# Top-32 selection of two heads in turns, with the check of the counts threaded through the next chunk maxima

## The chip, the cores and the metric

The kernel runs on one core of one Trainium2 chip. The metric is the device time of the whole program in microseconds (us), the median over runs. The engines are PE (TensorE: matrix products and transposes), DVE (VectorE), ACT (ScalarE), POOL (GpSimd) and SP (which only issues transfers). Each has its own instruction stream in program order, and they meet through semaphores.

## The reference, cut to what matters

One layer in three parts: a cross attention from 128 text rows to 2048 context rows with a state-space filter behind it, a banded self attention, and a mixture of 16 experts. The change lies in the first part, which is computed for 4 batches and 4 heads, so for 16 heads in all:

```python
scores = jnp.einsum('bthd,bghd->bhtg', Q, K) / np.sqrt(DH)     # 128 x 2048 for one head
topv, topi = jax.lax.top_k(scores, K_TOP)                      # K_TOP = 32
probs = jax.nn.softmax(topv, axis=-1)
attn = jnp.zeros_like(scores).at[bi, hi, ti, topi].set(probs)
attn_mean = attn.mean(axis=1)                                  # over the 4 heads of a batch
```

Beside it, the filter needs powers exp(dt * A * l) of complex numbers for 128 lags, as sines and exponentials of outer products.

## The kernel before, in words

The 16 heads go in order of batch; heads 2m and 2m+1 are pair m, so there are 8 pairs, and two pairs are a batch. For pair m the engines do this:

- PE multiplies queries and keys (`scores`, L1280), ACT copies the products from PSUM to SBUF (`scores`, L591) into one of five score buffers SC.
- DVE takes the 8 largest of each of 32 chunks of 64 scores (`chunk_maxima`, 32 MAX8 at L949), then finds the 32 largest of these 256 candidates (`threshold`: four MAX8 of 256 at L958, three MATCH_REPLACE8 at L961 between them). The 32nd is the head's threshold.
- `threshold` ends with two counts over the 128 partitions: how many candidates reach the threshold (L965), and in how many chunks the eighth one does (L966). A chunk of which all eight reach it could hide a ninth. `settle` (after the second head of a pair) brings the counts to one number: four reductions of 32 partitions each (L972), a maximum, a 32x32 transpose, a maximum; DVE reads the word into a register, and branches to an exact selection if it is above 64. With these inputs it never is. Then the memset at L985 signals `topk`.
- ACT waits for `topk` and runs `exponentials(m)` (L603): eight small instructions for the normalisation, then one exponential of 128 x 2048 for each head into W[0] and W[1] (L618). Each signals `e_done`.
- DVE runs `masked(i)` (L987): (score >= threshold) * exponential, 128 x 2048, one SCALAR_TENSOR_TENSOR at L990. It signals `masked`, which releases the score buffer and the next step.
- POOL adds the heads of a batch (`add_head`, L429 and L434, two TENSOR_TENSOR of 1024 columns for heads 1, 2 and 3 of a batch).

The powers of the filter are threaded through the same streams, one quarter q for each batch: ACT makes phases (`lag_turns`, `step_turns`), DVE rounds them (`whole(q)`, L997 and L998), POOL takes the fractions (`fractions(q)`, L442 and two at L444), ACT takes sines (L658, L659, each side of a table load), `lag_sizes` (L666) and `step_sizes` (L673), POOL multiplies (`magnitudes(q)`: L450, two transfers that swap the halves, L455, L456) and combines (`powers(q)`: L464 to L466; the last quarter is on DVE, `last_powers`, L1056 to L1058), PE contracts (`lags(q)`, L1338), and DVE gathers (`diagonal(q)`, L1004 and L1006). `step_turns(q)` waits until `lags(q-1)` has read the buffer that it writes.

The order on each engine is written out by hand. DVE, before, for heads i = 0 to 17: `chunk_maxima(i)`; `whole` (at i = 1, 6, 10, 14); `masked(i-2)`; `diagonal` (at i = 7, 11, 15); `threshold(i)`; and `settle` if i is odd. `last_powers` stands before `masked(14)`. POOL, for i = 2 to 17: `powers(i/4-1)` (at i = 4, 8, 12); `add_head(i-2)`; `fractions` (at i = 6, 10, 14); `magnitudes` (at i = 3, 7, 11, 15). At i = 16, `gains(0)` (L471, L472, which wait for ACT's `text_norm(0)` behind the last exponentials) stand before `add_head(14)`. ACT, for odd m: `exponentials(m-1)`, scores, attended rows, sines, sizes; for even m: exponentials, scores, context keys, `lag_turns`, `step_turns`, context keys.

Every instruction of `threshold` and `settle` is followed by a wait for its own end (`link`):

```python
def __call__(self, ins):
    self.n += 1
    ins.then_inc(self.sem, 1)
    self.eng.wait_ge(self.sem, self.n)
```

## Time and profile before

| what | value |
| --- | --- |
| time, median of 3 runs | 776.48 us (775.92 to 777.83) |
| the profiled execution, its own time | 782.62 us |
| its span | 780.8 us |
| PE, DVE, ACT, POOL busy over the span | 87%, 48%, 35%, 29% |
| DVE busy, 50 to 250 us | 43.41, 42.88, 45.64 and 42.67 us of each 50 |
| ACT busy, 50 to 250 us | 37.62, 42.06, 39.93 and 37.66 us of each 50 |
| POOL busy, 50 to 250 us | 43.67, 37.31, 35.36 and 38.00 us of each 50 |
| granted TensorE clock, 50 to 250 us | 0.67, 0.81, 0.70 and 0.66 |

The shares over the span mix three parts of the kernel. The selection lies in the first 255 us; the rest of the span belongs mainly to PE. Busy time says how full an engine is, not which one the others wait for.

### The profile page before, as it was taken

The numbers are of one execution on the slowest core, as the hardware profiler recorded it, in microseconds if no ns is written. First come the engines' busy times: TensorE is split into PE (matmuls) and PEld (weight loads), VectorE is DVE, ScalarE is ACT, GpSimd is POOL, SyncE is SP. The second block draws the span as 40 slices with busy tenths as digits, with TensorE's granted clock in tenths as the row PEclk, the third lists the DMA queues.
The fourth block names the chain that finished last, engine by engine and source line by source line (L and its number), as shares of the span: only waits on it lengthen the run. The fifth ranks groups of instructions, "written<-read, shape, count | busy, mean of one in ns | idle before, by whom it ended". The sixth has DMA issues, their size and how long they took to land.

```text
span 780.8 us, 10116 instructions
## 1 busy us (share of the span) xinstructions
PE 681.5 (87%) x3848; PEld 320.2 (41%) x3848; DVE 374.8 (48%) x1179; ACT 273.1 (35%) x580; POOL 227.5 (29%) x146
## 2 busy tenths in 40 slices
PE   4948659878478799999999999989799999999997
PEld 2314235334244354444444444545554333333343
DVE  5988879998997335561002341534662111001114
ACT  1867868879778110013120001545111001111010
POOL 2479767856957920000000000000140000000012
PEclk9976677868568899999999999999799999999999
DMA  9971320702704851006005014001958999999923
GB/s 289 292 280 40 107 82 7 263 1 83 281 0 161 264 222 40 1 0 216 0 7 209 0 39 177 1 1 47 384 199 303 389 375 346 372 373 369 382 80 126
DMA packets 63521, 132.94 MB, mean 170 GB/s; under 512 B 8368, under 2 KB 18544, under 8 KB 62960
## 3 DMA queue, kind: packets, MB, share of 16 engines
q1 hardware_dynamic: 59072, 122.91, 43.6%
q0 software_dynamic: 1920, 6.29, 2.8%
q10 hardware_dynamic: 2480, 3.08, 1.2%
q8 instruction: 30, 0.49, 0.3%
q14 instruction: 19, 0.16, 0.1%
HBM read 121.86 MB, written 8.32 MB: 167 GB/s over the span
## 4 chain that ended last, share of the span: by engine, by line
PE 63%; DVE 16%; POOL 9%; ACT 6%; issue 3%; DMA 2%; ACTq 0%; DVEq 0%; POOLq 0%
PE PS L1675 8%; PE PS L1650 7%; PE PS L1471 7%; PE PS L1491 7%; PE PS L1389 6%; PE PS L1243 4%; DVE KA L949 4%; PE PS L1508 4%; PE PS L1670 4%; PE PS L1655 4%; DVE AR L990 2%; PE PS L1505 2%; POOL TT L434 2%; PE PS L1319 1%; DVE V L958 1%
## 5 line engine op out<-in xcount | busy, mean ns | idle before, releaser
L415 POOL TENSOR_TENSOR RS<-VE,CST 128x1 f32<-128x1 f32 (+1 forms) x18 | 11.2, 621 | 268.7 <-DVE VE L912 266.4
L1276 PE MATMUL PS<-AR,WK 128*128 128x512 f32 x96 | 54.7, 726 | 17.3 <-DMA AR<-in_ctxT 17.3
L949 DVE MAX8 KA<-AR 128x8 f32<-128x64 f32 x512 | 66.4, 210 | 2.4 <-issue 2.0
L1214 DVE COPY AR<-PS 128x512 f32<-128x512 f32 (+1 forms) x9 | 5.9, 668 | 124.3 <-PE PS L1243 124.3
L1675 PE MATMUL PS<-AR,TT 128*32 128x512 f32 x512 | 60.3, 593 | 1.5 <-issue 1.4
L567 POOL DMA_INDIRECT AR<-expert_rows,SLU x8 | 8.3, 1034 | 181.0 <-DMA expert_rows<-XT 178.9
L1650 PE MATMUL PS<-AR 128*32 128x512 f32 x512 | 57.9, 594 | 0.9 <-ACT AR L863 0.6
L1471 PE MATMUL PS<-TT,AR 128*128 128x512 f32 (+2 forms) x144 | 55.5, 546 | 3.3 <-ACT TT L791 3.3
L1293 PE MATMUL PS<-AR,QT 32*128 32x512 f32 x128 | 43.3, 759 | 16.8 <-ACT AR L600 15.9
L1389 PE MATMUL PS<-AR 128*128 128x512 f32 x128 | 56.1, 594 | 0.3 <-DVE XT L1115 0.3
L1491 PE MATMUL PS<-AR 128*128 128x512 f32 x128 | 55.5, 593 | 0.9 <-ACT AR L800 0.9
L1319 PE MATMUL PS<-AR 128*128 128x384 f32 x128 | 49.6, 553 | 2.7 <-ACT AR L627 2.7
L1124 DVE TENSOR_TENSOR XT<-XT,PS 128x512 f32<-128x512 f32 x4 | 2.7, 687 | 86.6 <-PE PS L1491 86.6
L1276 PEld LDWEIGHTS PS<-AR,WK 128*128 128x128 f32 x96 | 21.5, 234 | 46.0 <-issue 37.7
L871 ACT ACTIVATE CCT<-PS 128x512 f32<-128x512 f32 x8 | 4.8, 597 | 101.1 <-PE PS L1655 101.1
L600 ACT ACTIVATE AR<-PS 128x512 f32<-128x512 f32 x64 | 34.3, 598 | 13.9 <-PE PS L1297 11.2
L1471 PEld LDWEIGHTS PS<-TT,AR 128*128 128x128 f32 x144 | 25.9, 190 | 31.9 <-issue 28.2
L1319 PEld LDWEIGHTS PS<-AR 128*128 128x128 f32 x128 | 27.6, 219 | 23.7 <-issue 6.6
L1491 PEld LDWEIGHTS PS<-AR 128*128 128x128 f32 x128 | 24.1, 190 | 30.8 <-issue 30.8
L1389 PEld LDWEIGHTS PS<-AR 128*128 128x128 f32 x128 | 24.1, 190 | 30.3 <-issue 30.2
L1675 PEld LDWEIGHTS PS<-AR,TT 128*32 128x32 f32 x512 | 17.4, 110 | 39.5 <-issue 38.2
L1650 PEld LDWEIGHTS PS<-AR 128*32 128x32 f32 x512 | 16.3, 110 | 36.6 <-issue 36.5
(290 smaller groups left out, 1205.7 us busy)
## 6 DMA issues: line engine op xcount, KB each, us to landing
AR<-in_w SPq DMA_DIRECT2D x32, 2048.0 KB, 12.4
AR<-in_ctxT SPq DMA_DIRECT2D x16, 768.0 KB, 8.1
AR<-in_ctx SPq DMA_DIRECT2D x16, 768.0 KB, 7.9
AR<-in_W SPq DMA_DIRECT2D x2, 4096.0 KB, 12.9
token_rows<-AR SPq DMA_DIRECT2D x1, 2560.0 KB, 11.0
X<-in_x SPq DMA_DIRECT2D x2, 1024.0 KB, 5.5
AR<-AR POOLq DMA_DIRECT2D x8, 256.0 KB, 3.4
AR<-in_W_film_in SPq DMA_DIRECT2D x4, 512.0 KB, 11.4
```

The lines of the kernel that those rows point to most:

```text
L600: eng.activation(SC[i % NSC][:, k * 512:(k + 1) * 512], PS[:, 2 * (k % 2) + j, :], ACT.Copy)\
L949: last = eng.max(CAND[0][:, n, :], s[:, n * G // NCH:(n + 1) * G // NCH])
L1243: return eng.transpose(dst, src, c("ident", rows)[:, 0:rows])
L1276: last = mm(PS[:, 4 + n % 2, :], WK[:, j, :], CXT[slot][:, j, :], start=j == 0, stop=j == KV - 1)
L1293: mm(PS[:, 2 * (k % 2) + j, :], QT[r, t], KT[b % 2][r, cols], start=True, stop=False)
L1319: last = mm(PS[:, 6, 0:DV], AT[:, g, :], CTX[:, g, :], start=g == 0, stop=g == GT - 1)
L1389: last = mm(PS[:, bank + j, :], CTT[:, k, b * T:(b + 1) * T], w[k][:, j * D:(j + 1) * D], start=k == 0, stop=k == KD - 1)
L1471: last = mm(PS[:, f % 8, lo * T:hi * T], W1[:, k, f * P:(f + 1) * P], TT[:, k, lo * T:hi * T], start=k == 0, stop=k == KD - 1)
L1491: last = mm(PS[:, b, :], GEL[:, f, b * T:(b + 1) * T], W2[:, f, :], start=f == 0, stop=f == HID // P - 1)
L1508: last = mm(PS[:, PROJ_BANK[n], :], WTR[:, "qk".index(a), k, u * P:(u + 1) * P], TT[:, k, :], start=k == 0, stop=k == KD - 1)
L1650: mm(PS[32 * q:32 * q + 32, 4 + j, :], XET[:, k, at_:at_ + 32], w[:, x, k, 512 * j:512 * j + 512], start=k == 0, stop=k == KD - 1)
L1675: last = mm(PS[32 * q:32 * q + 32, m % 2, :], HT[:, f, 32 * q:32 * q + 32], w[:, q // 2, f, :], start=f == 0, stop=f == F // P - 1)
```

## The change

Three edits on DVE and one on ACT:

- The order. For pair m, DVE now runs `chunk_maxima` of both heads, then `masked(2m-2)`, `whole(q)` if it is due, `masked(2m-1)`, `diagonal`, and then the selections of both heads. `whole(0)` stands behind the chunk maxima of heads 0 and 1 and before both selections.
- The selections in turns (`thresholds`). Head 0's instruction and head 1's alternate, and each waits only for the one of its own head, two before it. A second set of candidate buffers (LEFT, in KB) keeps them apart. The two counts of a head become one SCALAR_TENSOR_TENSOR of 256 columns with an accumulator: (candidate >= threshold) * "twice", a new constant row with 2 for the eighth of each chunk and 1 for the rest.
- The check. The four reductions stand behind the selections. The maximum, the transpose and the maximum stand behind the 4th, 8th and 12th chunk maximum of the next pair, and the reading of the word, the branch and the `topk` signal behind the 16th.
- ACT's `exponentials`: one Copy and one Ln of two columns take the place of two of one column each, and the last two Identity instructions no longer wait for each other.

```diff
--- before.py
+++ after.py
@@ -47,7 +47,7 @@
 
 CONST = {}
 _at = 0
-for _n, _w in [("ident", P), ("diag", 4), ("off1", 1), ("sign", 1), ("mhalf", 4), ("sel", B), ("one", 1), ("slot", FIRST),
+for _n, _w in [("ident", P), ("diag", 4), ("off1", 1), ("sign", 1), ("mhalf", 4), ("sel", B), ("one", 1), ("twice", 8), ("slot", FIRST),
                ("expert", E), ("spare", 2 * B), ("fxa", P), ("fxb", P), ("fkp", P), ("fkb", P), ("ga", P), ("gb", P),
                ("causal", P), ("tri", P), ("ones", P)]:
     CONST[_n] = (_at, _w)
@@ -93,6 +93,7 @@
     put("sign", 2 * top - 1)
     put("mhalf", -0.5)
     put("one", 1.0)
+    put("twice", np.where(np.arange(8) == 7, 2.0, 1.0)[None, :])
     put("sel", (q[:, None] % B == np.arange(B)[None, :]).astype(float))
     put("spare", NSLOT + P * np.arange(2 * B)[None, :] + q[:, None])
     return c
@@ -135,7 +136,7 @@
         MROW = sb("MROW", [P, G], bf16)
         ONEB = sb("ONEB", [P, P], bf16)
         V32 = sb("V32", [P, 4, TOPK])
-        FL = sb("FL", [P, 4])
+        FL = sb("FL", [P, 2])
         FQ = sb("FQ", [32, 4])
         SELB = sb("SELB", [P, B], bf16)
         FT = sb("FT", [32, 32])
@@ -217,7 +218,8 @@
         MA = at(36864, P, LA)
         KRAW = QT[:, :].rearrange("p (a b) -> p a b", b=P)
         KTD, DTE, RDEN = KA, KA, KP
-        CAND = [KA[:, n * 256:(n + 1) * 256].rearrange("p (a b) -> p a b", b=8) for n in range(2)]
+        CAND, LEFT = ([v[:, n * 256:(n + 1) * 256].rearrange("p (a b) -> p a b", b=8) for n in range(2)]
+                      for v in (KA, KB))
         RD = KP[:, :].rearrange("p (a b) -> p a b", b=LB)
         GRPS = P // 16
         GD = KB[:, :]
@@ -272,9 +274,15 @@
                 self.eng, self.sem, self.n = eng, S_[name], 0
 
             def __call__(self, ins):
+                self.after(self.put(ins))
+
+            def put(self, ins):
                 self.n += 1
                 ins.then_inc(self.sem, 1)
-                self.eng.wait_ge(self.sem, self.n)
+                return self.n
+
+            def after(self, n):
+                self.eng.wait_ge(self.sem, n)
 
 
         @block.sync
@@ -604,14 +612,14 @@
 
                 eng.wait_ge(S_["topk"], m + 1)
                 pair = [(i, V32[:, i % 4, :], SM[:, i % 4, :]) for i in (2 * m, 2 * m + 1)]
-                for i, v, a in pair:
-                    link(eng.activation(a[:, 0:1], v[:, 0:1], ACT.Copy, scale=-SCALE))
+                two = slice(2 * m % 4, 2 * m % 4 + 2)
+                link(eng.activation(SM[:, two, 0], V32[:, two, 0], ACT.Copy, scale=-SCALE))
                 for i, v, a in pair:
                     link(eng.activation(EV[:, :], v, ACT.Exp, bias=a[:, 0:1], scale=SCALE, accum_out=a[:, 1:2]))
+                link(eng.activation(SM[:, two, 2], SM[:, two, 1], ACT.Ln, scale=float(XH)))
                 for i, v, a in pair:
-                    link(eng.activation(a[:, 2:3], a[:, 1:2], ACT.Ln, scale=float(XH)))
-                for i, v, a in pair:
-                    link(eng.activation(a[:, 3:4], a[:, 2:3], ACT.Identity, bias=a[:, 0:1], scale=-1.0))
+                    last = link.put(eng.activation(a[:, 3:4], a[:, 2:3], ACT.Identity, bias=a[:, 0:1], scale=-1.0))
+                link.after(last)
                 for i, v, a in pair:
                     if i >= 2:
                         eng.wait_ge(S_["added"], sums_until(i - 2))
@@ -940,40 +948,67 @@
                 exact_link(eng.tensor_tensor(s, s, XW, ALU.add))
                 return exact_link.n - n0
 
-            def chunk_maxima(i):
+            def chunk_maxima(i, lo, hi):
 
                 s, per = SC[i % NSC], 512 * NCH // G
-                for k in range(GC):
-                    eng.wait_ge(S_["s_sb"], 2 * (GC * (i // 2) + k) + i % 2 + 1)
-                    for n in range(per * k, per * (k + 1)):
-                        last = eng.max(CAND[0][:, n, :], s[:, n * G // NCH:(n + 1) * G // NCH])
-                link(last)
-
-            def threshold(i):
-
-                v = V32[:, i % 4, :]
-                flat = [x.rearrange("p a b -> p (a b)") for x in CAND]
+                for n in range(lo, hi):
+                    if n % per == 0:
+                        k = n // per
+                        eng.wait_ge(S_["s_sb"], 2 * (GC * (i // 2) + k) + i % 2 + 1)
+                    last = eng.max(CAND[i % 2][:, n, :], s[:, n * G // NCH:(n + 1) * G // NCH])
+                return link.put(last)
+
+            def thresholds(m, found):
+
+                heads = []
+                for j in range(2):
+                    heads.append((V32[:, (2 * m + j) % 4, :], CAND[j].rearrange("p a b -> p (a b)"),
+                                  LEFT[j].rearrange("p a b -> p (a b)"), FL[:, j:j + 1]))
+                ready = found
                 for r in range(TOPK // 8):
-                    src = flat[min(r, 1)]
-                    link(eng.max(v[:, 8 * r:8 * r + 8], src))
+                    best = []
+                    for (v, c0, left, _), n in zip(heads, ready):
+                        link.after(n)
+                        best.append(link.put(eng.max(v[:, 8 * r:8 * r + 8], left if r else c0)))
                     if r == TOPK // 8 - 1:
                         break
-                    link(eng.match_replace(out=flat[1], in_to_replace=v[:, 8 * r:8 * r + 8], in_values=src,
-                                           imm_value=TAKEN))
-                th = v[:, TOPK - 1:TOPK]
-                a = FL[:, 2 * (i % 2):2 * (i % 2) + 2]
-                link(eng.tensor_scalar(flat[1], flat[0], th, 0.0, ALU.is_ge, ALU.add, accum_out=a[:, 0:1]))
-                link(eng.tensor_scalar(flat[1][:, 0:NCH], CAND[0][:, :, 7], th, 0.0, ALU.is_ge, ALU.add,
-                                       accum_out=a[:, 1:2]))
-
-            def settle(m):
+                    ready = []
+                    for (v, c0, left, _), n in zip(heads, best):
+                        link.after(n)
+                        ready.append(link.put(eng.match_replace(out=left, in_to_replace=v[:, 8 * r:8 * r + 8],
+                                                                in_values=left if r else c0, imm_value=TAKEN)))
+                for (v, c0, left, count_), n in zip(heads, best):
+                    link.after(n)
+                    last = link.put(eng.scalar_tensor_tensor(
+                        out=left.rearrange("p (a b) -> p a b", b=8), in0=c0.rearrange("p (a b) -> p a b", b=8),
+                        scalar=v[:, TOPK - 1:TOPK], in1=c("twice").unsqueeze(1).broadcast_to([P, NCH, 8]),
+                        op0=ALU.is_ge, op1=ALU.mult, accum_out=count_))
+                link.after(last)
+
+            def quadrant_counts():
 
                 for g in range(4):
                     last = eng.reduce_sum(FQ[:, g:g + 1], FL[32 * g:32 * g + 32, :], AX.X)
-                link(last)
-                link(eng.reduce_max(FT[:, 0:1], FQ[:, :], AX.X))
-                link(eng.transpose(FTT[:, :], FT[:, :]))
-                link(eng.reduce_max(FM[0:1, :], FTT[0:1, :], AX.X))
+                return link.put(last)
+
+            def largest_count(n):
+
+                link.after(n)
+                return link.put(eng.reduce_max(FT[:, 0:1], FQ[:, :], AX.X))
+
+            def count_row(n):
+
+                link.after(n)
+                return link.put(eng.transpose(FTT[:, :], FT[:, :]))
+
+            def count_word(n):
+
+                link.after(n)
+                return link.put(eng.reduce_max(FM[0:1, :], FTT[0:1, :], AX.X))
+
+            def settle(m, n):
+
+                link.after(n)
                 counted = eng.value_load(FM[0:1, 0:1], min_val=0, max_val=2 * NCH * 9)
                 with eng.If(counted > 2 * TOPK):
                     eng.wait_ge(S_["coef"], 1)
@@ -1058,24 +1093,37 @@
                 tt(PM, PM, PW, sub).then_inc(S_["powers"], 1)
 
             link(eng.memset(FT[:, :], 0.0))
-            for i in range(NT + 2):
-                q, k = divmod(i, 4)
-                if i < NT:
-                    chunk_maxima(i)
-                if i == 1:
+            for m in range(NPH):
+                q, late = divmod(m, 2)
+                if m:
+                    chunk_maxima(2 * m, 0, 4)
+                    word = largest_count(word)
+                    chunk_maxima(2 * m, 4, 8)
+                    word = count_row(word)
+                    chunk_maxima(2 * m, 8, 12)
+                    word = count_word(word)
+                    chunk_maxima(2 * m, 12, 16)
+                    settle(m - 1, word)
+                    found = [chunk_maxima(2 * m, 16, NCH)]
+                else:
+                    found = [chunk_maxima(0, 0, NCH)]
+                found.append(chunk_maxima(2 * m + 1, 0, NCH))
+                if m == 0:
                     whole(0)
-                if k == 2 and 1 <= q < 4:
+                if m:
+                    masked(2 * m - 2)
+                if q and late:
                     whole(q)
-                if i == NT:
-                    last_powers()
-                if 2 <= i < NT + 2:
-                    masked(i - 2)
-                if k == 3 and q:
+                if m:
+                    masked(2 * m - 1)
+                if q and late:
                     diagonal(q - 1)
-                if i < NT:
-                    threshold(i)
-                if i % 2 and i < NT:
-                    settle(i // 2)
+                thresholds(m, found)
+                word = quadrant_counts()
+            settle(NPH - 1, count_word(count_row(largest_count(word))))
+            last_powers()
+            masked(NT - 2)
+            masked(NT - 1)
 
             def modulate(b):
```

## Rows read from the trace of the kernel before

**Rows 1.** Page, costliest groups: line, count, busy us, mean ns of one.

```profile
L949 DVE MAX8 KA<-AR 128x8 f32<-128x64 f32 x512 | 66.4, 210 | 2.4 <-issue 2.0
```

**Rows 2.** DVE timeline, pair 0: start us, length us, instruction, idle time before.

```profile
34.39 0.43 DVE L958 MAX8 V<-KA 128x8 f32<-128x256 f32 x1
...
37.81 0.48 DVE L965 TENSOR_SCALAR_CACHE_REDUCE KA<-KA,V 128x256 f32<-128x256 f32 x1
...
38.64 4.15 DVE L949 MAX8 KA<-AR 128x8 f32<-128x64 f32 x32
...
48.94 0.62 DVE L972 TENSOR_REDUCE FQ<-FL 32x1 f32<-32x4 f32 x4
...
51.47 0.06 DVE L985 MEMSET EV<- 128x1 f32 x1 [1.29 <-issue]
```

**Rows 3.** ACT timeline, 51 to 228 us, same columns.

```profile
51.57 0.44 ACT L608 ACTIVATE SM<-V 128x1 f32<-128x1 f32 x2 [7.15 <-DVE EV L985]
...
78.36 0.48 ACT L608 ACTIVATE SM<-V 128x1 f32<-128x1 f32 x2
...
124.72 1.28 ACT L658 ACT_TABLE_LOAD   x1
...
135.41 0.42 ACT L608 ACTIVATE SM<-V 128x1 f32<-128x1 f32 x2
...
161.13 0.43 ACT L608 ACTIVATE SM<-V 128x1 f32<-128x1 f32 x2
...
212.71 0.44 ACT L608 ACTIVATE SM<-V 128x1 f32<-128x1 f32 x2 [2.20 <-DVE EV L985]
...
227.88 1.06 ACT L658 ACTIVATE AR<-AR 128x1024 f32<-128x1024 f32 x1 [4.29 <-POOL AR L444]
```

**Rows 4.** POOL timeline, 39 to 253 us, same columns.

```profile
39.70 1.27 POOL L488 TENSOR_TENSOR AR<-AR,KP 128x512 f32<-128x512 f32 x1
...
88.06 2.35 POOL L455 TENSOR_TENSOR AR<-AR 128x1024 f32<-128x1024 f32 x1 [4.62 <-ACT AR L673]
...
98.70 2.34 POOL L466 TENSOR_TENSOR AR<-AR 128x1024 f32<-128x1024 f32 x1
...
132.50 2.36 POOL L450 TENSOR_TENSOR AR<-AR 128x1024 f32<-128x1024 f32 x1 [0.19 <-ACT AR L666]
...
138.56 2.36 POOL L456 TENSOR_TENSOR AR<-AR 128x1024 f32<-128x1024 f32 x1
...
147.25 2.36 POOL L466 TENSOR_TENSOR AR<-AR 128x1024 f32<-128x1024 f32 x1
...
199.37 2.35 POOL L466 TENSOR_TENSOR AR<-AR 128x1024 f32<-128x1024 f32 x1
...
218.84 4.39 POOL L442 TENSOR_TENSOR AR<-AR 128x1024 f32<-128x1024 f32 x1 [5.62 <-DVE AR L998]
...
236.49 2.35 POOL L450 TENSOR_TENSOR AR<-AR 128x1024 f32<-128x1024 f32 x1
...
252.81 7.15 POOL L434 TENSOR_TENSOR TT<-TT,AR 128x1024 f32<-128x1024 f32 x2 [2.23 <-DVE AR L990]
```

**Rows 5.** DVE timeline, 114 to 250 us, same columns.

```profile
114.41 2.35 DVE L990 SCALAR_TENSOR_TENSOR AR<-AR,V 128x2048 f32<-128x2048 f32 x1 [2.41 <-ACT AR L618]
...
139.99 3.08 DVE L990 SCALAR_TENSOR_TENSOR AR<-AR,V 128x2048 f32<-128x2048 f32 x1 [0.61 <-ACT AR L618]
...
166.55 2.35 DVE L990 SCALAR_TENSOR_TENSOR AR<-AR,V 128x2048 f32<-128x2048 f32 x1
...
216.80 0.69 DVE L997 TENSOR_SCALAR AR<-AR 128x1024 f32<-128x1024 f32 x1
...
218.67 2.35 DVE L990 SCALAR_TENSOR_TENSOR AR<-AR,V 128x2048 f32<-128x2048 f32 x1
...
243.35 2.63 DVE L1056 TENSOR_TENSOR AR<-AR 128x1024 f32<-128x1024 f32 x1 [3.83 <-DMA AR<-AR]
...
249.37 3.36 DVE L990 SCALAR_TENSOR_TENSOR AR<-AR,V 128x2048 f32<-128x2048 f32 x1
```

## Prediction

> **What bounds the kernel now.** I read the busy time by stage first (the table above). Between 50 and 250 us DVE is busy 43 to 46 us of each 50, so it looks like the bound, and the change takes work from DVE. But ACT is busy 38 to 42 and POOL 35 to 44, and full engines don't tell who waits for whom. So I read the timelines of ACT and POOL beside DVE's.
>
> The reader is to see three things. ACT, not DVE, is late at most pairs: its exponentials begin at 135.41 and 161.13 with no idle time before them, which means that ACT was busy until then. Only at 212.71 did it sit waiting for `topk`, 2.20 us [rows 3]. DVE for its part waited for an exponential: 2.41 us before `masked(4)` at 114.41, 0.61 before `masked(6)` at 139.99 [rows 5]. And what keeps ACT busy is a loop through all engines: whole (DVE), fractions (POOL), sines and sizes (ACT), magnitudes (POOL), exponentials (ACT), masked (DVE), powers (POOL), lags (PE), step turns (ACT), exponentials, masked, whole. At 227.88 ACT waited 4.29 us for the fractions [rows 3], at 88.06 POOL waited 4.62 us for the sizes [rows 4]. DVE's saving counts only where this loop has slack; what counts is what the new order puts into it.
>
> **A lock between DVE and POOL.** L442 takes 4.39 us at 218.84, where `masked(12)` had begun at 218.67 and ended at 221.02; the same shape takes 2.36 at 132.50 and at 138.56 with no such neighbour [rows 4, 5]. So POOL stood still for 2.03. The other way round, `masked(6)` was issued at 139.99 while L456 ran to 140.92, and took 3.08 for 2.35 [rows 4, 5]. Whoever starts first finishes, the other waits. The small DVE instructions of the selection overlapped POOL everywhere and kept their lengths. The Trainium skill (SBUF — State Buffer, § Who interferes with whom) says the same, an exclusive lock for DVE instructions with two SBUF inputs or in a two-port mode, and adds that a tensor_scalar that writes an accumulator isn't among them; this speaks against the change, which turns counts of that free kind into ones with two inputs. No row shows a short instruction of the new kind.
>
> **The parts, and their price on DVE.**
>
> Selections in turns. Seven linked instructions of one head take 37.81 - 34.39 = 3.42 us [rows 2]. A chunk maximum alone takes 210 ns [rows 1], but 32 without waits take 4.15 us, 130 ns each [rows 2]: they overlap by 80 ns, and a linked one pays about 35 ns more for its wait. I take 115 ns for each of 14 boundaries: two heads in 6.84 - 1.6 = 5.2. Bounds: nothing saved (6.8), or all of that.
>
> Counts. Before 38.64 - 37.81 = 0.83 a head [rows 2]. After, one instruction of 256 columns and an accumulator; nearest by size is L965 (0.48, [rows 2]), by kind L990. I take 0.95 for the two by size, and the lock by kind: each may wait for POOL's instruction in progress, up to 2.36, and POOL may slip in between the two. Bounds: no lock, or 2.3 more for the second.
>
> Check. Before 51.47 - 48.94 = 2.53 [rows 2]. After: reductions 0.65; 16 maxima and the three small ones 2.5; the reading and branch still about 1.2 early and 1.0 later. `topk` comes 4.4 behind the selections rather than 2.5, but 2.1 of it is work that was due anyway. Gain on DVE 0.4.
>
> Exponentials. Two Copies take 0.42 [rows 3], so one saves 0.2; the Ln likewise; the last link 0.15. Together 0.57 for a pair, on ACT, which is in the loop. This is the change's real gain.
>
> **The sum.** Four stretches, from one masked product to another.
>
> A, up to `masked(4)`. `whole(0)` now comes at 38.6, where POOL's 1.27 us instructions run back to back until 40.97 [rows 4]; its two instructions wait for one each and end at 42.7. Selections 5.2: 47.9. But the fractions of quarter 0 now run on POOL from 42.8 to 49.75 (three of 2.3), and the counts wait for them: 50.7. Reductions 0.65, maxima 2.5, reading 1.2: `topk(0)` at 55.1, where it was 51.47 [rows 2]. ACT had stood idle 7.15 us for it [rows 3], so all of it counts: +3.6 less 0.6, ACT 3.0 late until the next exponentials (78.36 becomes 81.4). `topk(1)`: 48 maxima 6.25, the two masked products among POOL's instructions 6.5, selections 5.2, a wait of 1, then 5.3: 79.4, or 81.7 if an `add_head` half goes between the counts. The step sizes end 2.4 later, so L455 moves from 88.06 to 90.45, or to 92.45 behind `masked(3)`. From there to the end of powers it took 101.04 - 88.06 = 12.98 [rows 4] with a masked product in the way; without one 11.2 (4.7, and 149.61 - 143.07 = 6.5 [rows 4, 5]), plus 0.7 to 0.9 for counts: 102.4 to 104.4. Less 0.6 for the exponentials: +0.7 to +2.7, I take +1.7.
>
> B, `masked(4)` to `masked(8)`, 52.14 before [rows 5]. With `masked(4)` starting at 0: whole now stands behind it and not ahead, ends at 4.1 (1.87, [rows 5]). `masked(5)` takes the lock before the fractions wake, exactly the case of 218.84: from there to 227.84 they take 9.0 [rows 3, 4], so 13.25. ACT's table load is done in its idle time; lag sizes at 13.25 + 132.42 - 124.72 - 1.28 = 19.7. From L450 to the end of L456 8.42 [rows 4]: 28.1. The exponential for `masked(6)` is ready at 13.25 + (135.41 - 124.72 - 1.28) + 4.58 - 0.57 = 26.7, and the product waits for L456: 28.1, end 30.4. Before it was 143.07 - 114.41 = 28.7. Now `masked(7)` stands right behind it and takes the lock from powers: 2.1, and then 6.5: 39.0; before 35.2 [rows 4]. From there to the exponentials 161.13 - 149.61 = 11.5 [rows 3, 4], and 4.0: `masked(8)` at 54.5. B is +2.4.
>
> C, `masked(8)` to `masked(12)`, 52.12 before [rows 5]. The same 39.0; from the end of L466 (201.72) ACT was ready at 212.71 - 2.20 = 210.51, 8.8 later [rows 3, 4]: 47.8. DVE has `topk` by 44.1 to 46.4, so the old wait for it is gone. With 4.0 more: 51.8. C is -0.3.
>
> D, `masked(12)` to the end of `add_head(14)`, before 259.96 - 218.67 = 41.3 [rows 4, 5]. Lag sizes 19.7; the swapped halves land 243.35 - 236.49 = 6.9 after L450's start [rows 4, 5], at 26.6; L456 holds the lock until 28.1; `last_powers` ends at 31.9. `text_norm(0)` now comes at the same moment (25.2 + 4.0 + 1.9 + 0.8), where before the two gains were through before `masked(14)`. From 31.9 all take turns at one lock: gains 2.5 (as 1.27 at 39.70, [rows 4]), two masked products 4.6, `add_head(14)` 4.7: 43.7. D is +2.4. Behind it everything moves along with POOL's sum.
>
> A to D: +6.2. The profiled execution took 782.62 us (span 780.8), so 788.8 by its own time; it stands 0.8% above the median, which gives 782.7 beside 776.48. What a measurement of this kernel can tell from no change is 0.3%, 2.3 us.
>
> **Rivals.**
>
> 1. No overlap: an instruction in turns costs what a linked one does. Speaks for it: no row shows two unlinked ones of 256 columns. Against: rows 1 and 2. Then a pair's selections take 1.6 more: A +1.6, and DVE becomes late in B and C by 0 to 1.2 and 0.2 to 2.4, and POOL instructions fall between the counts: about +5 in all, 787.7. The skill (VectorE: DVE Perf Modes, § The DRAIN you can't avoid) says it: eight copies took the same time with a semaphore behind each and behind the last alone.
>
> 2. The short counts take no lock. `topk(0)` at 53.2 (+1.7), nothing else late: A is 1.2 earlier at powers, -1.8 with the exponentials; the rest stays: +2.7, 779.2, on the edge of what can be told.
>
> 3. POOL's L464 gets the lock ahead of `masked(7)` and `masked(11)`: 2.1 less in B and in C, +2.0, 778.5, no change. Against it: `masked(13)`-like followers start 80 ns before their forerunner ends, and L434 at 252.81 took 7.15 behind just such a one [rows 4, 5].
>
> 4. The other side, faster: DVE is the bound, and POOL and ACT have room. Each pair then gives 1.6 + 0.7 + 0.4 = 2.7, 8 pairs 22: 755; a part of it gives 765 to 774. It decides if ACT stands idle before its exponentials at most pairs. For it: 7.15 and 2.20 us of such waits, and DVE's fullness. Against it: 135.41 and 161.13.
>
> **Numbers.** Forecast 0.47 (its own range 779.5 to 786), rival 1 0.15, rival 2 0.12, rival 3 0.11, rival 4 0.15. Slower: 0.47 + 0.15 and half of rival 2, 0.68. Same: the other half and rival 3, 0.17. Faster 0.15. The range leaves out rival 4 and the far end of rival 1: 776 to 789.5.
>
> **What the new profile would show.** If right: DVE idle for several us before `masked(4)`, `masked(8)` and `masked(12)`; the first `topk` memset near 55; L442 near 4.4 at all three later quarters; L464 near 4 at two of them; ACT idle before its sines in each of quarters 1 to 3; selections of a pair near 5.2 plus waits at the counts. Wrong if the selections stay at 6.8, if the counts never wait, if ACT waits for `topk` more than now, or if the stretch from `masked(4)` to `masked(8)` is under 52.

## The result and the profile after

The changed kernel takes 780.13 us (median of 6 runs, 779.33 to 782.51); the kernel before, run beside it, 776.85 (6 runs, 775.92 to 777.83). The ratio is 1.0042, 95% interval 1.0025 to 1.0060: slower by 3.3 us, 1.9 to 4.7. A second measurement of the same pair on another chip gave 1.0044 (1.0029 to 1.0060). The forecast was slower, 782.7 beside 776.48 (+6.2), with its own range from 779.5 to 786 and the wide one from 776 to 789.5.

The two profiled executions can't be compared by their spans (780.8 and 777.5): in the one of before, 500 us behind the change, 64 matmuls (L1675, from 758.07) took 12.4 us, and in the changed one 7.0. The place to compare is the start of 32 matmuls of `context_rows` for the last batch, which multiply its attention by the context once ACT has copied the last of it (L627 before); I call it the mark. Here it is in the PE timeline of the kernel before (start us, length us, instruction, idle time before):

```profile
269.34 10.59 PE L1319 MATMUL PS<-AR 128*128 128x384 f32 x32 [0.69 <-ACT AR L627]
```

and of the changed kernel, with the row ahead of it:

```profile
267.78 3.59 PE L1291 MATMUL PS<-CST,TT 128*128 128x128 f32 x16 [2.51 <-POOL TT L442]
272.06 10.59 PE L1367 MATMUL PS<-AR 128*128 128x384 f32 x32 [0.69 <-ACT AR L635]
```

The mark moved from 269.34 to 272.06, by 2.72. Up to the expert part nothing adds to it: its first matmul starts at 572.21 before and at 574.93 after, again 2.72. Within the expert part single executions differ by more than this (just before those 64 matmuls the two are 1.2 us apart), so one profile can't show the whole difference at the end. The 2.72 lie within the interval of the medians, and they arise in the selection part.

The changed kernel's DVE timeline, pair 0 (to compare with [rows 2]; the last row is `masked(0)`):

```profile
37.72 0.67 DVE L1032 TENSOR_SCALAR AR<-AR 128x1024 f32<-128x1024 f32 x1
38.43 2.17 DVE L1033 TENSOR_SCALAR AR<-AR 128x2048 f32<-128x2048 f32 x1
40.52 0.74 DVE L972 MAX8 V<-KA 128x8 f32<-128x256 f32 x2
...
45.51 1.25 DVE L982 SCALAR_TENSOR_TENSOR KB<-KA,V,CST 128x256 f32<-128x256 f32 x1
...
46.68 2.55 DVE L982 SCALAR_TENSOR_TENSOR KB<-KA,V,CST 128x256 f32<-128x256 f32 x1
...
49.27 0.61 DVE L991 TENSOR_REDUCE FQ<-FL 32x1 f32<-32x2 f32 x4
...
53.43 0.06 DVE L1020 MEMSET EV<- 128x1 f32 x1 [1.15 <-issue]
...
59.52 2.67 DVE L1025 SCALAR_TENSOR_TENSOR AR<-AR,V 128x2048 f32<-128x2048 f32 x1
```

The two heads' selections, fourteen instructions, take 45.51 - 40.52 = 5.0 us where one head took 3.42. The two counts (L982) take 3.8 us. The memset that signals `topk(0)` is at 53.43, 2.0 later than before, though in this execution the first chunk maximum began 0.6 earlier (29.60 and 30.20).

DVE, the masked products from `masked(4)` on and `last_powers` (to [rows 5]; L1033 is the larger half of whole):

```profile
113.31 2.35 DVE L1025 SCALAR_TENSOR_TENSOR AR<-AR,V 128x2048 f32<-128x2048 f32 x1 [6.78 <-ACT AR L626]
...
116.30 1.23 DVE L1033 TENSOR_SCALAR AR<-AR 128x2048 f32<-128x2048 f32 x1
117.44 2.35 DVE L1025 SCALAR_TENSOR_TENSOR X<-AR,V,X 128x2048 f32<-128x2048 f32 x1
...
139.93 3.78 DVE L1025 SCALAR_TENSOR_TENSOR AR<-AR,V 128x2048 f32<-128x2048 f32 x1 [0.49 <-ACT AR L626]
143.64 2.34 DVE L1025 SCALAR_TENSOR_TENSOR X<-AR,V,X 128x2048 f32<-128x2048 f32 x1
...
167.74 2.35 DVE L1025 SCALAR_TENSOR_TENSOR AR<-AR,V 128x2048 f32<-128x2048 f32 x1 [2.54 <-ACT AR L626]
...
219.28 2.35 DVE L1025 SCALAR_TENSOR_TENSOR AR<-AR,V 128x2048 f32<-128x2048 f32 x1
...
245.95 2.61 DVE L1091 TENSOR_TENSOR AR<-AR 128x1024 f32<-128x1024 f32 x1 [8.21 <-DMA AR<-AR]
```

DVE now stands idle 6.78 us ahead of `masked(4)` and 8.21 ahead of `last_powers`, where it was 2.41 and 3.83. POOL (to [rows 4]):

```profile
89.47 2.35 POOL L463 TENSOR_TENSOR AR<-AR 128x1024 f32<-128x1024 f32 x1 [4.77 <-ACT AR L681]
...
98.43 2.34 POOL L474 TENSOR_TENSOR AR<-AR 128x1024 f32<-128x1024 f32 x1
...
117.61 4.40 POOL L450 TENSOR_TENSOR AR<-AR 128x1024 f32<-128x1024 f32 x1 [7.41 <-DVE AR L1033]
121.96 4.67 POOL L452 TENSOR_TENSOR AR<-AR 128x1024 f32<-128x1024 f32 x2
...
139.20 2.36 POOL L464 TENSOR_TENSOR AR<-AR 128x1024 f32<-128x1024 f32 x1
143.80 4.01 POOL L472 TENSOR_TENSOR AR<-AR 128x1024 f32<-128x1024 f32 x1 [2.24 <-DVE AR L1025]
147.88 1.97 POOL L473 TENSOR_TENSOR AR<-AR 128x1024 f32<-128x1024 f32 x1
...
255.45 7.17 POOL L442 TENSOR_TENSOR TT<-TT,AR 128x1024 f32<-128x1024 f32 x2
```

L450 was issued 0.17 us behind `masked(5)` (117.44) and takes 4.40; its like in the kernel before, L442, began at 116.90, at the end of `masked(4)`, and took 2.35. So the fractions end 13.3 us behind the start of `masked(4)`, where it was 9.5. L472 stands behind `masked(7)` (143.64) in the same way and takes 4.01 rather than 1.97. ACT (to [rows 3]) shows it from the other side, waiting for the fractions in each of the quarters 1 to 3 and for `topk` only at the first pair:

```profile
53.52 0.21 ACT L616 ACTIVATE SM<-V 128x2 f32<-128x2 f32 x1 [9.57 <-DVE EV L1020]
...
126.66 1.06 ACT L666 ACTIVATE AR<-AR 128x1024 f32<-128x1024 f32 x1 [1.75 <-POOL AR L452]
...
136.02 0.20 ACT L616 ACTIVATE SM<-V 128x2 f32<-128x2 f32 x1
...
163.82 0.20 ACT L616 ACTIVATE SM<-V 128x2 f32<-128x2 f32 x1
...
215.37 0.20 ACT L616 ACTIVATE SM<-V 128x2 f32<-128x2 f32 x1
...
232.63 1.06 ACT L666 ACTIVATE AR<-AR 128x1024 f32<-128x1024 f32 x1 [6.99 <-POOL AR L452]
```

And DVE by groups, 29 to 240 us (busy us, mean ns of one, idle time before and what ended it), before

```profile
L965 DVE TENSOR_SCALAR_CACHE_REDUCE KA<-KA,V 128x256 f32<-128x256 f32 x16 | 7.7, 479 | 0.6
L966 DVE TENSOR_SCALAR_CACHE_REDUCE KA<-KA,V 128x32 f32<-128x32 f32 x16 | 4.3, 270 | 0.6
...
L990 DVE SCALAR_TENSOR_TENSOR AR<-AR,V 128x2048 f32<-128x2048 f32 x7 | 18.1, 2583 | 6.2 <-ACT AR L618 6.2
```

and after

```profile
L982 DVE SCALAR_TENSOR_TENSOR KB<-KA,V,CST 128x256 f32<-128x256 f32 x16 | 27.7, 1768 | 0.0
L1025 DVE SCALAR_TENSOR_TENSOR AR<-AR,V 128x2048 f32<-128x2048 f32 x7 | 19.6, 2803 | 11.7 <-ACT AR L626 11.6
```

The 32 accumulating counts cost 7.7 + 4.3 = 12.0 us, the 16 new ones 27.7: 1768 ns each on average. What DVE doesn't spend on selections it spends in these and in waiting for ACT (6.2 became 11.6).

### The profile page after: what moved, and what is told of

The parts are those of the page before. It is cut to its first block, busy times and chain, and to the rows that moved or that the text cites. A ratio compares the mean times of both kernels' runs of the same rounds, so it can differ in the third digit from the quotient of the medians.

```text
span 777.5 us, 10045 instructions
## 1 busy us (share of the span) xinstructions
PE 673.9 (87%) x3848; PEld 318.3 (41%) x3848; DVE 375.7 (48%) x1147; ACT 268.4 (35%) x564; POOL 234.2 (30%) x146
## 4 chain that ended last, share of the span: by engine, by line
PE 61%; ACT 10%; POOL 10%; DVE 5%; issue 3%; DMA 2%; POOLq 0%; DVEq 0%; ACTq 0%
PE PS L1698 7%; PE PS L1519 7%; PE PS L1539 7%; PE PS L1437 6%; PE PS L1723 6%; PE PS L1291 4%; PE PS L1556 4%; PE PS L1703 4%; PE PS L1718 3%; PE PS L1553 2%; PE PS L1324 2%; POOL TT L442 2%; POOL AR L452 1%; DVE AR L1025 1%; PE PS L1367 1%
## 5 line engine op out<-in xcount | busy, mean ns | idle before, releaser
L1324 PE MATMUL PS<-AR,WK 128*128 128x512 f32 x96 | 56.3, 744 | 17.2 <-DMA AR<-in_ctxT 17.2
L1723 PE MATMUL PS<-AR,TT 128*32 128x512 f32 x512 | 56.4, 592 | 0.0
L1367 PE MATMUL PS<-AR 128*128 128x384 f32 x128 | 49.2, 549 | 2.7 <-ACT AR L635 2.7
L1519 PEld LDWEIGHTS PS<-TT,AR 128*128 128x128 f32 x144 | 25.9, 190 | 31.9 <-issue 28.2
L1698 PEld LDWEIGHTS PS<-AR 128*32 128x32 f32 x512 | 16.2, 110 | 35.2 <-issue 35.2
```

Of the source, the lines that this page charges most:

```text
L1324: last = mm(PS[:, 4 + n % 2, :], WK[:, j, :], CXT[slot][:, j, :], start=j == 0, stop=j == KV - 1)
L1367: last = mm(PS[:, 6, 0:DV], AT[:, g, :], CTX[:, g, :], start=g == 0, stop=g == GT - 1)
L1519: last = mm(PS[:, f % 8, lo * T:hi * T], W1[:, k, f * P:(f + 1) * P], TT[:, k, lo * T:hi * T], start=k == 0, stop=k == KD - 1)
L1698: mm(PS[32 * q:32 * q + 32, 4 + j, :], XET[:, k, at_:at_ + 32], w[:, x, k, 512 * j:512 * j + 512], start=k == 0, stop=k == KD - 1)
L1723: last = mm(PS[32 * q:32 * q + 32, m % 2, :], HT[:, f, 32 * q:32 * q + 32], w[:, q // 2, f, :], start=f == 0, stop=f == F // P - 1)
```

## The experiments

Each was measured in 5 to 12 executions beside the kernel before on the same chip. The table gives the places of three masked products and the mark, in one profiled execution each; two profiles of one kernel (the changed one, rows 2 and 3) differ by 0.6 us at the first maximum, by up to 1.4 at a masked product and by 0.03 at the mark. Distance to before at the mark and by the ratio differ by up to 2.2 us (e9), so a smaller difference that only one of them shows is weak. The last column is the ratio of the times to the kernel before; its medians were 783.11 us for e1 to e4, 782.3 for e5 to e8, 783.03 for e9 to e11 and 777.26 for e12, so 0.001 is 0.8 us.

| kernel | first maximum | masked(4) | masked(8) | masked(12) | mark | ratio (95%) |
| --- | --- | --- | --- | --- | --- | --- |
| before | 30.20 | 114.41 | 166.55 | 218.67 | 269.34 | 1 |
| changed | 29.60 | 113.31 | 167.74 | 219.28 | 272.06 | 1.0042 (1.0025 to 1.0060) |
| changed, again (e5) | 30.24 | 114.67 | 167.62 | 219.19 | 272.09 | 1.0044 (1.0029 to 1.0060) |
| e1 whole ahead | 29.96 | 114.43 | 166.44 | 217.94 | 268.76 | 0.9990 (0.9971 to 1.0008) |
| e2 free counts | 29.96 | 111.40 | 164.52 | 216.12 | 268.91 | 1.0000 (0.9987 to 1.0014) |
| e3 before + ACT edit | 30.37 | 114.51 | 166.69 | 218.85 | 269.25 | 0.9995 (0.9980 to 1.0011) |
| e4 second product late | 29.52 | 114.94 | 167.82 | 220.61 | 272.67 | 1.0059 (1.0039 to 1.0080) |
| e6 order of before | 30.00 | 117.28 | 169.88 | 222.01 | 272.74 | 1.0028 (1.0011 to 1.0045) |
| e7 heads one by one | 29.73 | 117.52 | 171.58 | 225.26 | 277.88 | 1.0104 (1.0089 to 1.0119) |
| e8 = e1 + e2 | 30.30 | 112.29 | 164.62 | 214.41 | 263.98 | 0.9958 (0.9945 to 0.9972) |
| e9 = e8 + powers unblocked | 30.22 | 113.06 | 162.61 | 211.30 | 261.88 | 0.9876 (0.9854 to 0.9898) |
| e10 check in one piece | 29.90 | 112.65 | 165.65 | 218.20 | 270.90 | 1.0009 (0.9993 to 1.0026) |
| e11 ACT edit undone | 29.93 | 114.83 | 169.52 | 221.68 | 274.74 | 1.0088 (1.0066 to 1.0110) |
| e12 = e9 + e10 | 29.86 | 111.69 | 161.45 | 210.89 | 261.69 | 0.9875 (0.9855 to 0.9896) |

**e1, whole ahead of both masked products** (in the changed kernel):

```diff
                 if m == 0:
                     whole(0)
-                if m:
-                    masked(2 * m - 2)
                 if q and late:
                     whole(q)
                 if m:
+                    masked(2 * m - 2)
                     masked(2 * m - 1)
```

> The changed kernel, whole(q) moved ahead of masked(2m-2) in pairs 3, 5 and 7; nothing else. Theory (the loop, not DVE, sets the time): the rounding then stands in DVE's idle time before the product, so the fractions end 11.4 us after the start of masked(4q) instead of 13.3 to 13.4, and everything behind them in the loop comes 1.9 us earlier, in each of three quarters: masked(4) to masked(8) 52.5 us instead of 54.4, and 4 to 6 us off the time, 774.5 to 776 us. Rival (the new waits of the counts for POOL cost the 3.3 us): the stretches stay at 54.4 and 51.5, and the time at 780.

The mark came 3.3 us earlier than in the changed kernel, 4.1 by the ratio (4 to 6 expected). From `masked(4)` to `masked(8)` it is 52.0, as before, and from `masked(12)` to the mark 50.8, as before's 50.7. L450 still meets the lock, but from 2.5 us behind the start of `masked(4)` on, not from 4.3, so the fractions end 11.5 behind it and not 13.3:

```profile
116.93 4.33 POOL L450 TENSOR_TENSOR AR<-AR 128x1024 f32<-128x1024 f32 x1 [5.51 <-DVE AR L1025]
```

`masked(8)` to `masked(12)` did not get shorter (51.5): there whole now starts at 216.08, some 6 us after `topk`, and no ACT wait is left in front of it. DVE, held up at its counts, is the late one there. So with whole ahead the changed kernel is where before is (0.6 ahead at the mark). That doesn't make the place of whole the only cause: e2 and e10 bring the ratio back to about 1 as well, each by another edit, and the order of before (e6) does not.

**e2, the counts as they were** (accumulating tensor_scalar, two for a head, both heads in turns):

```diff
-                    last = link.put(eng.scalar_tensor_tensor(
-                        out=..., in0=..., scalar=v[:, TOPK - 1:TOPK], in1=c("twice")...,
-                        op0=ALU.is_ge, op1=ALU.mult, accum_out=count_))
+                    ready.append(link.put(eng.tensor_scalar(left, c0, v[:, TOPK - 1:TOPK], 0.0, ALU.is_ge, ALU.add,
+                                                            accum_out=count_[:, 0:1])))
+                for j, ((v, c0, left, count_), n) in enumerate(zip(heads, ready)):
+                    link.after(n)
+                    last = link.put(eng.tensor_scalar(left[:, 0:NCH], CAND[j][:, :, 7], v[:, TOPK - 1:TOPK], 0.0,
+                                                      ALU.is_ge, ALU.add, accum_out=count_[:, 1:2]))
```

> The changed kernel with the two old accumulating counts of each head (256 and 32 columns, one tensor input), in turns, in place of the one with two inputs. Theory: they never wait for POOL, so a pair's counts take about 1.3 us instead of 2.8 to 3.7, topk(0) comes 2.3 us earlier, and the stretch up to masked(4) is 2 to 3 us shorter; from masked(4) to masked(8) and on to masked(12) the loop hides DVE and nothing changes (54.4, 51.5). Time 777 to 778. Rival (the counts' waits are what made the kernel slower everywhere): the later stretches shrink too, and the time falls below 776.

Measured: 3.15 us less at the mark, and 3.3 by the ratio, 1.9 to 3.3 of it ahead of `masked(4)`. The later stretches are those of the changed kernel, as expected (53.1 beside 52.95 in e5, and 51.6), the time a little better than expected. Its counts, while POOL formed the fractions:

```profile
124.09 0.47 DVE L983 TENSOR_SCALAR_CACHE_REDUCE KB<-KA,V 128x256 f32<-128x256 f32 x1
...
124.48 0.48 DVE L983 TENSOR_SCALAR_CACHE_REDUCE KB<-KA,V 128x256 f32<-128x256 f32 x1
...
124.88 0.27 DVE L987 TENSOR_SCALAR_CACHE_REDUCE KB<-KA,V 128x32 f32<-128x32 f32 x1
...
125.08 0.27 DVE L987 TENSOR_SCALAR_CACHE_REDUCE KB<-KA,V 128x32 f32<-128x32 f32 x1
```

and the changed kernel's at the same place:

```profile
126.01 0.90 DVE L982 SCALAR_TENSOR_TENSOR KB<-KA,V,CST 128x256 f32<-128x256 f32 x1
...
126.84 2.57 DVE L982 SCALAR_TENSOR_TENSOR KB<-KA,V,CST 128x256 f32<-128x256 f32 x1
```

Four of the old form go in 1.3 us, two of the new in 3.4. The lock is taken even by an instruction of 256 columns, and the old form is free of it, as the Trainium skill says (SBUF — State Buffer, § Who interferes with whom); the trace agrees.

**e3, the ACT edit alone, in the kernel before:** one Copy and one Ln for two heads, no wait behind the first Identity.

> The kernel before with the shorter exponentials of ACT alone. Theory: 0.5 to 0.6 us less between topk and the first exponential in every pair, of which only pairs in which ACT is the late one pass it on; 1.5 to 2 us in all, 774.9 to 775.4 us. Rival (DVE is the bound before): no change within 0.5 us.

No gain: 0.09 us at the mark. `masked(6)` was issued at 139.50 rather than 139.99, met POOL's L462 (138.69, 2.35) and ended where it had ended. Its two rows, the changed product and the first of the powers:

```profile
139.50 3.71 DVE L996 SCALAR_TENSOR_TENSOR AR<-AR,V 128x2048 f32<-128x2048 f32 x1
```

```profile
138.69 2.35 POOL L462 TENSOR_TENSOR AR<-AR 128x1024 f32<-128x1024 f32 x1
143.28 1.97 POOL L470 TENSOR_TENSOR AR<-AR 128x1024 f32<-128x1024 f32 x1 [2.24 <-DVE AR L996]
```

Before, the powers began at 143.15. The half microsecond went into the wait at the lock; the expectation (1.5 to 2 us less) was wrong. The rival had the time, but the row names the lock and not a full DVE.

**e4, the second product behind the thresholds, at every pair** (`masked(2m-1)` moved behind `thresholds(m, found)`):

> The changed kernel with masked(2m-1) moved behind the selections of pair m; nothing else. Theory: nothing holds the lock when POOL starts the fractions and the powers, so L450 and L472 fall from 4.4 and 4.0 us to 2.35 and 1.97; the fractions end 11.3 us after the start of masked(4q), the powers 2 us earlier still: masked(4) to masked(8) about 51 us, masked(8) to masked(12) 50 to 51, and 775 to 777 us, since DVE's product may then wait 2 us for POOL. Rival (the lock only shifts POOL's work and costs nothing net): 780.

Both lock waits went, as expected: L450 took 2.35 and L472 1.97. The time didn't fall: 3.33 us behind before at the mark, 4.6 by the ratio, more than the rival had. `masked(5)`, at 126.94, now came so late that POOL waited for it, L464 ran until 142.4, and `masked(6)` took 4.76:

```profile
129.37 4.68 POOL L437 TENSOR_TENSOR TT<-AR,X 128x1024 f32<-128x1024 f32 x2 [3.16 <-DVE X L1025]
```

```profile
139.85 4.76 DVE L1025 SCALAR_TENSOR_TENSOR AR<-AR,V 128x2048 f32<-128x2048 f32 x1 [0.68 <-ACT AR L626]
```

What had been a lock wait on POOL came back as one on DVE. The expectation allowed for that one, and left out POOL's wait of 3.16 for the late product.

**e5** is the changed kernel a second time, on the chip of e6 to e8.

> The changed kernel once more, beside the kernel before on this chip. The ratio measured first was 1.0042 (+3.3 us). Theory (the 3.3 us come from the first 268 us, where the traces agree to a few tenths from run to run): the same ratio, 1.003 to 1.006. Rival (the difference was one of the two chips or of the PE-bound rest): a ratio within 0.002 of 1.

The mark is the same. `masked(4)` to `masked(8)` took 52.95 here and 54.43 in the first profile. Between them lie twelve matmuls of one context step, first profile and second:

```profile
154.19 7.49 PE L1324 MATMUL PS<-AR,WK 128*128 128x512 f32 x12
```

```profile
155.57 6.00 PE L1324 MATMUL PS<-AR,WK 128*128 128x512 f32 x12
```

The mean granted clock from 140 to 168 us was 0.77 and 0.88; in both, PE had stood idle for 5.4 us ahead of the 64 short matmuls in front of these. In effect the slower matmuls used up the 1.4 us by which the first profile was ahead at `masked(4)` (0.6 of them from before the first maximum): `masked(8)` and `masked(12)` are 0.1 apart.

**e6, the order of before** (whole and `masked(2m-2)` ahead of the second head's maxima, all else changed):

> The changed kernel with the old places of whole and of the two masked products: whole(q) and masked(2m-2) between the chunk maxima of the two heads, masked(2m-1) behind them. Selections in turns, the new counts, the drawn check and the shorter exponentials stay. Theory (the order is what costs): the fractions and the powers no longer find the lock taken; from masked(4) to masked(8) 51 to 52.5 us, the last stretch 2 us shorter; the counts still wait for POOL and make DVE late before masked(12), so not all comes back: within 2 us of the kernel before. Rival (counts or check cost, not the order): +3 us as for the changed kernel.

From `masked(12)` to the mark 50.73, as before. But `masked(4)` is 2.6 later than in e5: `masked(3)` at 92.55 now meets POOL's L463 and takes 3.30, and `topk(1)` comes at 82.2 instead of 77.7. So the new order is worth 2.6 us ahead of `masked(4)`, and costs 2.2 behind `masked(12)`. At the mark this kernel is 3.4 behind before and 0.65 behind e5, by the ratio 2.2 behind before and 1.3 ahead of e5, with intervals that overlap. The expectation (within 2 us of before) is not borne out, and the two orders aren't told apart. e1 is better than either: it keeps the masked products behind the maxima, and takes only whole out from between them.

**e7, one head's selection after the other**, each instruction waiting for the one ahead:

```diff
-                for r in range(TOPK // 8):
-                    best = []
-                    for (v, c0, left, _), n in zip(heads, ready):
+                for (v, c0, left, _), n in zip(heads, found):
+                    link.after(n)
+                    for r in range(TOPK // 8):
+                        link(eng.max(v[:, 8 * r:8 * r + 8], left if r else c0))
...
```

> The changed kernel with the selections of the two heads one after the other and every instruction linked, as before; the new counts stay. Theory: 14 instructions of a pair take 6.8 us instead of 5.0; this shows before masked(12), where DVE had no idle time, and at topk(0) and topk(1), but not before masked(4) and masked(8), where DVE waited: +2 to +4 us against the changed kernel, so 1.007 to 1.010 of before. Rival (DVE is nowhere the bound): no change against the changed kernel.

5.8 us more at the mark than in e5, 4.7 by the ratio, above the 2 to 4 expected; the turns are worth that. By groups, 29 to 240 us:

```profile
L971 DVE MAX8 V<-KB 128x8 f32<-128x256 f32 x48 | 20.5, 428 | 1.7
```

```profile
L972 DVE MAX8 V<-KB 128x8 f32<-128x256 f32 x48 | 17.8, 411 | 0.0
```

A linked instruction waits 35 ns (1.7 us over 48), and is 17 ns longer. The rest of the saving is that in turns the next one starts some 70 ns before this one ends: in pair 0 two maxima ran from 40.52 to 41.26, and the next row begins at 41.19. The Trainium skill has two cases that bear on this: VectorE: DVE Perf Modes, § The DRAIN you can't avoid, measured nothing saved without semaphores, and § Two Vector instructions with no wait between them lets one that isn't held start earlier. The trace agrees with the second.

**e8, e1 and e2 together.**

> Both mendings at once: whole(q) ahead of masked(2m-2), and the two old counts, free of the lock, in turns. Theory: alone, the first left masked(8) to masked(12) at 51.5 because DVE, slowed by the counts, became the late one there, and the second left the fractions late. Together both stretches fall: masked(4) to masked(8) 51 to 52, masked(8) to masked(12) 49 to 50, and topk(0) is 2.2 us earlier: 3.5 to 6 us faster than the kernel before, 0.992 to 0.996. Rival (each mending gives its own and no more): 0.998 to 0.9995.

8.1 us ahead of the changed kernel at the mark, and 5.4 ahead of before; 3.3 by the ratio, just short of the 3.5 expected. In this profile the matmuls at the mark took 12.35 us instead of 10.59, which leaves 3.6 behind them. But those of e3 took 12.46 beside a ratio of 0.9995, so it stays open whether that loss belongs to the kernel. The third stretch fell from e1's 51.5 and e2's 51.6 to 49.8: with free counts and whole ahead DVE is not late there any more.

**e9, e8 with the powers unblocked** at the two pairs where L472 met the lock:

```diff
-                if m:
+                if m and m not in (4, 6):
                     masked(2 * m - 1)
...
                 thresholds(m, found)
+                if m in (4, 6):
+                    masked(2 * m - 1)
```

> The kernel of e8 with one more edit: in the pairs m = 4 and 6 the second masked product of the pair before, masked(2m-1), stands behind the pair's thresholds instead of ahead of the chunk maxima, so that it no longer takes the lock while GpSimd forms the powers L474 and the step that follows. Theory (that product's lock is what holds GpSimd up at 143.8 in the changed kernel, 4.01 for L472 against 2.36 alone): masked(4) to masked(8) falls by about 2 us against e8 (52.3 to 50.2), masked(8) to masked(12) by 1.5 (49.8 to about 48.3), the parts ahead of masked(4) and behind masked(12) stay within 0.5; ratio to the kernel before 0.991 to 0.993. Rival (as in e4 VectorE becomes the late one, its product standing in the selections' way): the wait ahead of masked(8) is gone and nothing is gained, ratio 0.995 to 0.997.

The fastest, with e12: 773.66 us beside 783.03, an interval below 1 and below e8's, and better than expected. L472 at its place in e8 and in e9 (free it takes 1.97, not the 2.36 of the expectation):

```profile
141.03 4.01 POOL L472 TENSOR_TENSOR AR<-AR 128x1024 f32<-128x1024 f32 x1 [2.24 <-DVE AR L1028]
```

```profile
141.78 1.97 POOL L472 TENSOR_TENSOR AR<-AR 128x1024 f32<-128x1024 f32 x1 [2.24 <-DVE AR L1028]
```

The second stretch fell by 2.8 us against e8 and the third by 1.1. DVE didn't become the late one: with free counts it still waited 3.04 us for ACT ahead of `masked(6)`. The outer parts moved more than the 0.5 I had allowed, `masked(4)` 0.85 and the last stretch 1.0 the wrong way. The mark is 7.5 ahead of before's, the first matmul of the expert part 7.4 (564.77); the medians differ by 9.4, and what causes the rest, behind that matmul, isn't shown.

**e10, the check in one piece** behind the selections of its own pair, in the changed kernel:

> The changed kernel with the check not drawn: each pair's counts are checked in one piece right behind its selections, and the next chunk maxima stand behind the check. Theory (the drawn check only moves work on VectorE and is no cause of the 3.3 us): the first thresholds leave about 2 us sooner (the memset ahead of them at 51.4 instead of 53.4), so start to masked(4) falls by 1 to 2 us; masked(4) to masked(8) and masked(12) to the end, which the lock of the whole product sets, stay within 0.3; masked(8) to masked(12) rises by 0.4; against the changed kernel -0.5 to -1.5 us, ratio to the kernel before 1.002 to 1.004. Rival (the drawn check is what made the change slow): ratio back at 1.000.

1.2 us less at the mark, 2.7 by the ratio. Ahead of `masked(4)` it gains, as expected; the third stretch gives 1.0 back. Drawing the check through the maxima costs rather than saves here; it is a part of the 3.3. How large a part is open: by the mark under half, while the ratio's interval takes in 1, as the rival has it.

**e11, the ACT edit undone** in the changed kernel:

> The changed kernel with ScalarE's Copy and Ln turned back to the form of before (the edit that e3 tried alone). By the prediction's sum ScalarE then comes 0.57 us later at each pair's thresholds, and as in this kernel ScalarE's phase gives the time of masked(4), masked(8) and masked(12), the three gaps between them would be longer by up to 0.57 each: +1 to +1.5 us against the changed kernel, ratio to the kernel before 1.005 to 1.0065. Rival (absorbed as in e3, by a wait that ends at GpSimd): no change, 1.003 to 1.0045.

It cost more than expected: 2.7 us at the mark, 3.6 by the ratio. Its thresholds at the pair of `masked(4)`:

```profile
110.31 0.44 ACT L616 ACTIVATE SM<-V 128x1 f32<-128x1 f32 x2
...
112.80 2.00 ACT L626 ACTIVATE AR<-AR,SM 128x2048 f32<-128x2048 f32 x1
```

```profile
109.39 0.21 ACT L616 ACTIVATE SM<-V 128x2 f32<-128x2 f32 x1
...
111.28 2.00 ACT L626 ACTIVATE AR<-AR,SM 128x2048 f32<-128x2048 f32 x1
```

From the first Copy to the exponential 2.49 and 1.89, 0.6 a pair. Part of it is carried on: the first Copy is 0.32 later (53.84 and 53.52; the first maximum was 0.33 later too), the one two pairs on 0.92. Eight pairs of 0.6 would make 4.8; about half of that, 2.3 of the 2.7, is there at the mark. So in the changed kernel about half of what ACT saves is passed on, in the kernel before nothing was (e3).

**e12, e9 and e10 together.**

> The kernel of e9 with e10's edit: the counts are checked in one piece behind each pair's selections, and the next chunk maxima follow. If the cost of the drawn check adds up with the rest as it did in the changed kernel (1.2 us at the matmuls behind the last norm), this kernel is about 1 us faster than e9: ratio to the kernel before 0.985 to 0.988. Rival: with the lock out of the way VectorE is nearer to being the late one, and the 1.2 us for which it waits for the read at each pair come back (start to masked(4) 1 us less, masked(4) to masked(12) 1 to 2 us more): ratio 0.988 to 0.991.

As e9, by the ratio; it lies in the expected range only because e9 itself had come out lower. `masked(4)` comes 1.4 earlier (1.0 from the first maximum on), the three stretches behind it take 1.2 more, and the mark is 0.2 earlier: that is the rival's mechanism. A reading that no run isolates: waiting for the count is idle time of DVE, and behind `masked(4)` DVE has none to give.

## Why the prediction was right, point by point

**Stretch B**, forecast 54.5, measured 54.43, and by its steps: fractions end 13.3 behind `masked(4)` (13.25 in the sum), lag sizes 19.7 (19.7), L464 28.25 (28.1), exponential for `masked(6)` 26.6 (26.7), powers 39.0 (39.0), from there to the next thresholds 11.5 (11.5). The second profile (e5) has the same 39.0 up to the powers (114.67 to 153.65) and 52.95 in all: its matmuls behind them were 1.5 us faster. So the loop up to the powers is right, and that the whole stretch agreed to 0.1 in the first profile is luck: the +2.4 forecast for it came out as +2.3 and as +0.8. **C**: powers 38.9 (39.0), 51.5 (51.8). **D**: last powers 31.8 (31.9), end of `add_head(14)` 43.3 (43.7). For D the cause is shown: with whole ahead of the products (e1) or in its old place (e6) the last stretch is back at 50.8 and 50.7, from 52.8. In B e1 takes 1.9 off the end of the fractions and 1.8 off the powers (37.2 behind `masked(4)`). e9 showed what the second product costs the powers, 2.1 us (35.2 for e8's 37.2).

**Stretch A** is the term that was mis-sized: +1.7 forecast, -1.1 measured in the first profile (-0.5 from the first maximum on) and +0.3 in the second. It is most of the reason why the forecast was 6.2 for a measured 2.7 to 3.3 by the first profile, and as much of it as B by the second. `whole(0)` met one POOL instruction and not two, and ended at 40.6, not 42.7; the counts behind it ended at 49.2, not 50.7; `topk(0)` was at 53.4, not 55.1. `topk(1)` came at 77.0 (79.4 to 81.7): the 1.7 was carried on, and no `add_head` half went between the counts (1.35 and 1.48). And a count delayed POOL by 0.2 or less (L472 2.15, L473 2.03, for 1.97) where I had 0.7 to 0.9. Powers ended at 100.8, not at 102.4 to 104.4.

**The selections** at 5.0 (5.2) and the overlap of instructions in turns: right, shown by e7. The check's gain of 0.4 on DVE: none; e10 shows a loss. **ACT's 0.57**, called the change's real gain: by itself it gave nothing (e3), in the changed kernel 2.7 (e11). The sum takes it off wherever it follows ACT; its worth hangs on the order around it.

**The signs.** DVE idle ahead of `masked(4)` and `masked(8)`, 6.78 and 2.54 us, came; ahead of `masked(12)` it had none. L450 took 4.4 at all three later quarters, L472 4.01 and 3.21, and ACT waited for the fractions at each of them; none of the signs of being wrong came. Of the kernel before the prediction says that ACT waited for `topk` only at 212.71; its own row at 51.57 has 7.15 us of such a wait.

**The rivals.** Rival 1 is out (e7), and its price of about 5 us is near the 4.7 that e7 cost. Rival 2's +2.7 is nearer to the measured +3.3 than the forecast's +6.2, but its mechanism is out: the counts take the lock, 2.57 against 0.48 (e2). Had they not, 3.2 us would have been saved. Rival 3 didn't happen, `masked(7)` has the lock first. Rival 4 is out: DVE waits for ACT 11.6 us at the first products of the pairs, not less than before.

At the mark the parts, each changed alone, give: turns -5.8, ACT edit -2.7; place of whole (against e1's, not against before's) +3.3, counts +3.2, drawn check +1.2. They sum to -0.8 and not to +2.7: they aren't additive, as e3 against e11 shows too. By the ratio e1, e2 and e10 each bring the kernel back to 1 within their intervals (0.9990, 1.0000, 1.0009). So the 3.3 us have no single cause: the edits share one loop, and which of them is charged depends on what else is mended.

## What to carry to other kernels

Follow the loop through the engines step by step with lengths from the trace; here the steps through DVE, POOL and ACT came out within 0.4 us, though DVE as the fullest engine suggested a gain; where PE's clock enters, one stretch moved by 1.5 us between two executions. Before a large two-input instruction is put next to another, ask what wakes on the other engine at the end of the first: at each place seen here the second took the lock ahead of it. The same edit was worth 0 or 2.7 us by the order around it, so parts of a change are to be tried both alone and left out.

## What had not been expected of the hardware

A two-input count of 256 columns waits for POOL's instruction as a large one does (2.57 us, where one with POOL idle took 0.48, at 126.42 in e4), but POOL lost only 0.2 us or less to each. Instructions of the two heads in turns start some 70 ns inside each other's length: fourteen in 5.0 us. The read of a counted value and the branch leave DVE idle for 1.15 us with the check drawn ([rows 2] have 1.29), and for 0.90 to 0.48 at later pairs, with further chunk maxima due. The granted clock of one short stretch differed between two executions of the same kernel (0.77 and 0.88, 140 to 168 us): it was 0.50, the lower of PE's two levels (1.2 GHz of 2.4), while PE stood idle for 5.4 us and behind that until 158 us in the one and until 156 in the other, though the other's matmuls had begun 1.4 us later. That made twelve matmuls 1.5 us longer, and the mark no later.
